# Local attention of a transformer step: strips of TensorE's array for the scores, one addition on GpSimd

## The reference, cut to what matters

```python
q = (x @ WQ_w + WQ_b).reshape(Bx, Lx, nh, d)
k = (x @ WK_w + WK_b).reshape(Bx, Lx, nh, d)
ak = (ax @ WK_w + WK_b).reshape(Bx, 1, nh, d)
av = (ax @ WV_w + WV_b).reshape(Bx, 1, nh, d)
pad_k = jnp.pad(k, ((0, 0), (1, 1), (0, 0), (0, 0)))
k_shift = jnp.stack([pad_k[:, t:Lx + t] for t in range(3)], axis=3)
K = jnp.concatenate([akb, k_shift], axis=3)
V = jnp.concatenate([avb, k_shift], axis=3)
scores = jnp.einsum('blhd,blhjd->blhj', q, K) / jnp.sqrt(jnp.float32(d))
alphas = jax.nn.softmax(scores, axis=-1)
att = jnp.einsum('blhj,blhjd->blhd', alphas, V).reshape(Bx, Lx, nh * d)
return att @ WO_w + WO_b
```

## Time and profile before

| | us |
|---|---|
| median of three runs | 1703.72 (1702.59 to 1705.21) |
| the profiled execution, its own time | 1703.39 |
| its span | 1701.6 |
| TensorE busy in the span | 1564.6 (92%) |
| VectorE busy | 827.5 (49%) |
| ScalarE busy | 662.9 (39%) |
| GpSimd busy | 94.7 (6%) |

### The profile page before, as it was taken

The page is one execution under the profiler, slowest core; times in us unless marked ns, Lnnn a source line. Parts: engine busy times, 40 slices in busy tenths (PEclk is TensorE's granted clock), DMA queues, the critical chain, the costliest instruction groups (busy, mean ns, idle before and its releaser), DMA issues. The chain is left out here.

```text
span 1701.6 us, 32009 instructions
## 1 busy us (share of the span) xinstructions
PE 1564.6 (92%) x11861; PEld 1250.0 (73%) x11862; DVE 827.5 (49%) x2926; ACT 662.9 (39%) x2449; POOL 94.7 (6%) x135
## 2 busy tenths in 40 slices
PE   7999989879999899999999999879999999866995
PEld 5666555537777799999999999638888888753663
DVE  2777668755445334444444444473333333565223
ACT  3211112125555145555555455314344434523442
POOL 0000000000000000000000000010000000003662
PEclk9988889889999999999999999859999999967998
DMA  4000000000000300000000000010000000001113
GB/s 146 1 1 1 0 1 1 1 0 1 1 1 1 100 1 2 2 1 2 2 2 1 2 2 1 1 31 21 20 26 20 27 14 2 1 1 47 41 43 92
DMA packets 27731, 28.05 MB, mean 16 GB/s; under 512 B 2293, under 2 KB 22234, under 8 KB 27450
## 3 DMA queue, kind: packets, MB, share of 16 engines
q1 hardware_dynamic: 20970, 16.70, 3.4%
q0 software_dynamic: 2496, 5.12, 1.0%
q10 hardware_dynamic: 4112, 4.19, 0.8%
HBM read 21.35 MB, written 4.65 MB: 15 GB/s over the span
## 5 line engine op out<-in xcount | busy, mean ns | idle before, releaser
L1457 PE MATMUL spare<-identb 128*128 128x128 bf16 x3166 | 218.2, 219 | 0.0
L1457 PEld LDWEIGHTS spare<-identb 128*128 128x128 bf16 x3166 | 201.7, 103 | 4.3
L292 PE MATMUL sc<-headsel,prod 128*128 128x128 f32 x1024 | 164.6, 315 | 0.7 <-DVE prod L437 0.7
L292 PEld LDWEIGHTS sc<-headsel,prod 128*128 128x128 f32 x1024 | 142.6, 218 | 26.7 <-issue 24.3
L1055 DVE TENSOR_TENSOR_SCAN narg<-rz,pre_n 128x16 f32<-128x16 f32 x256 | 47.9, 187 | 219.9 <-PE pre_n L952 218.9
L990 ACT ACTIVATE ghid<-gh_ps,cols 128x128 f32<-128x128 f32 x512 | 144.3, 366 | 12.9 <-PE gh_ps L891 12.7
L891 PE MATMUL gh_ps<-hist,w 128*128 128x128 f32 x1024 | 137.5, 275 | 0.6 <-ACT ghid L990 0.6
L900 PE MATMUL gy_ps<-w2e,ghid 128*128 128x128 f32 x1024 | 136.8, 276 | 0.6
L900 PEld LDWEIGHTS gy_ps<-w2e,ghid 128*128 128x128 f32 x1024 | 124.4, 191 | 3.0 <-issue 3.0
L891 PEld LDWEIGHTS gh_ps<-hist,w 128*128 128x128 f32 x1024 | 126.0, 188 | 0.8 <-DVE hist L1063 0.8
L952 PE MATMUL pre_r<-hist,gru_w 128*128 128x128 f32 x512 | 118.1, 312 | 0.7 <-DVE hist L1063 0.5
(11 more groups left out here) (374 smaller groups left out, 2664.1 us busy)
## 6 DMA issues: line engine op xcount, KB each, us to landing
w<-in_L_ffn_W SPq DMA_DIRECT2D x1, 2048.0 KB, 9.6
raw<-in_L_ffn_wg SPq DMA_DIRECT2D x8, 256.0 KB, 2.9
raw<-in_L_ffn_wu SPq DMA_DIRECT2D x8, 256.0 KB, 2.8
raw<-in_L_ffn_wd SPq DMA_DIRECT2D x8, 256.0 KB, 2.7
wqkv<-in_L_attn_Wqkv SPq DMA_DIRECT2D x1, 1536.0 KB, 6.4
mrow<-mt SPq DMA_DIRECT2D x4, 256.0 KB, 2.4
y_top<-yrow SPq DMA_DIRECT2D x4, 256.0 KB, 5.4
y_next<-yrow ACTq DMA_DIRECT2D x4, 256.0 KB, 6.1
```

The source lines that it names most:

```text
L292: mm = nc.tensor.matmul(sc[:, :, :, :].rearrange("p i j h -> p (i j h)"), prod[u % 2][:, j, P * i:P * i + P], headsel[:, P - 2 * k:2 * P - ...
L1457: nc.tensor.matmul(spare[:, 0:P], n.identb[:, :], n.identb[:, :], start=True, stop=True)
```

## The change

The block is written anew. `x` is kept as `xB`, one batch after the other, so neighbours are adjacent columns. The work goes in 32 steps (`STEPS`): 4 groups of two batches (512 columns) by 8 chunks. Per step:

- One projection of queries and one of keys, 512 columns each.
- One VectorE product of 128x1536 elements, for three keys instead of four: the conditioning key is folded into the query weights once at the start (`cond_keys`, `gq`) and costs two multiplications of 256 columns a group (`cond_scores`).
- Three score multiplications (`scores`). Now `headsel`, 32 columns wide, is the loaded operand and the product the moving one with 512 columns. Each writes its own strip of 32 partitions of one PSUM tile, `sc`, and so uses its own 32 columns of the array. All 8 chunks add to the same tile.
- The softmax comes once a group, for all 16 heads: ScalarE copies the scores to SBUF, TensorE turns them (`turn_scores`), VectorE works on 64 to 256 elements a partition, TensorE turns the parts back (`turn_probs`).
- Three spreads of 512 columns with 96, 96 and 48 rows, three VectorE terms (`weighted`), 10 steps behind the scores (`LAG`), so the loop has 43 rounds: 10 without spreads, 22 with everything (the last two of them without projections) and 11 with spreads and output alone.
- GpSimd adds two of the terms (`pair_terms`). The third goes to TensorE by itself: `project_out` makes two multiplications of 512 columns a step, with the same weights. The conditioning value's term is folded into the output weights (`av_wo`), two multiplications of 256 columns a group.

In the linear attention only the source of the residual `x` changes. The core of the diff:

```diff
+                    nc.scalar.activation(n.xB[:, 512 * g:512 * g + 512], turn[g % 2][:, :, :].rearrange("p i t -> p (i t)"),
...
-    HALF = TOK // 2
-    HB = HALF // P
-    SH = B
-    KW = HALF + 2 * SH
-    UNITS = 2 * NC
-    J = 4
+    J = 3
+    GB = 2
+    W = GB * T
+    NG = B // GB
+    STEPS = NG * NC
+    LAG = NC + 2
+    NK = LAG + 2
+    R = 32
+    HR = HEADS
...
+        headsel = sb("headsel", [P, 2 * R])
+        pick = sb("pick", [2 * 3 * HR, J, NC, 2, HD], BF16)
...
+        pj = [ps(f"pj{i}", [P, W]) for i in range(2)]
+        bc = [ps(f"bc{i}", [P, W]) for i in range(2)]
+        sc = ps("sc", [P, W])
+        y_ps = ps("y_ps", [P, W])
+        tok = ps("tok", [P, W])
+        tr = ps("tr", [2 * 3 * HR, 2, W], BF16)
...
+                def pair_terms(u):
+                    if not 0 <= u < STEPS:
+                        return
+                    pool.wait_ge(term_done, J * u + 2)
+                    if u >= 2:
+                        pool.wait_ge(y_part, u - 1)
+                    nc.gpsimd.tensor_tensor(pair[u % 2][:, :], term[u % 2][:, 0, :], term[u % 2][:, 1, :],
+                                            ALU.add).then_inc(pair_done, 1)
+
+                for u in range(STEPS):
+                    pair_terms(u)
...
+                def project(s, i):
+                    if s >= STEPS:
+                        return
+                    g, c = divmod(s, NC)
+                    k = 2 * s + i
+                    if k >= 2:
+                        pe.wait_ge(proj_kept, k - 1)
+                    w = (wq, wk)[i]
+                    nc.tensor.matmul(pj[k % 2][:, :], w[:, P * c:P * c + P], n.xB[:, W * g:W * g + W],
+                                     start=True, stop=True).then_inc(proj_done, 1)
...
+                def scores(s, j):
+                    if s >= STEPS:
+                        return
+                    g, c = divmod(s, NC)
+                    if j == 0 and c == 0 and g >= 1:
+                        pe.wait_ge(sc_kept, GB * g)
+                    if j == 0:
+                        pe.wait_ge(prod_v, s + 1)
+                    at = R * (j + 1)
+                    mm = nc.tensor.matmul(sc[at:at + R, :], headsel[:, R - 2 * c:2 * R - 2 * c], prod[s % 2][:, j, :],
+                                          start=(c == 0), stop=(c == NC - 1))
+                    if j == J - 1:
+                        mm.then_inc(score_done, 1)
...
+                def turn_scores(g):
+                    pe.wait_ge(sc_kept, GB * (g + 1))
+                    if g == 0:
+                        pe.wait_ge(gcol_kept, 1)
+                    else:
+                        pe.wait_ge(p0_kept, g)
+                    for i in range(4):
+                        mm = nc.tensor.transpose(tok[:, P * i:P * i + P], sc_sb[:, P * i:P * i + P], n.ident[:, :])
+                    mm.then_inc(sc_turned, 1)
...
+                def turn_probs(g):
+                    pe.wait_ge(parts_done, g + 1)
+                    if g >= 1:
+                        pe.wait_ge(turned_kept, g)
+                    for i in range(4):
+                        nc.tensor.transpose(tr[:, 0, P * i:P * i + P],
+                                            parts[:, J * i:J * i + 2, :, :].rearrange("p j k r -> p (j k r)"), n.identb[:, :])
+                        nc.tensor.transpose(tr[0:3 * HR, 1, P * i:P * i + P],
+                                            parts[:, J * i + 2, :, :].rearrange("p k r -> p (k r)"), n.identb[:, :])
+                    for i in range(4):
+                        mm = nc.tensor.transpose(tok[0:HEADS, P * i:P * i + P], prob0[:, i, :], n.ident[:, :])
+                    mm.then_inc(turned, 1)
...
+                def spread_probs(u, j):
+                    if not 0 <= u < STEPS:
+                        return
+                    g, c = divmod(u, NC)
+                    k = J * u + j
+                    if j == 0 and c == 0:
+                        pe.wait_ge(turned_kept, g + 1)
+                    if k == 0:
+                        pe.wait_ge(const_a, 10)
+                        pe.wait_ge(av_kept, 2)
+                    if k >= 2:
+                        pe.wait_ge(term_done, k - 1)
+                    k0 = 2 * 3 * HR if j < 2 else 3 * HR
+                    nc.tensor.matmul(bc[k % 2][:, :], pick[0:k0, j, c, :, :].rearrange("r h d -> r (h d)"),
+                                     probT[0:k0, j // 2, :], start=True, stop=True).then_inc(spread, 1)
+
+                def project_out(u):
+                    if not 0 <= u < STEPS:
+                        return
+                    g, c = divmod(u, NC)
+                    if c == 0:
+                        if g >= 1:
+                            pe.wait_ge(y_kept, g)
+                        else:
+                            pe.wait_ge(wav_kept, 1)
+                        pe.wait_ge(p0_kept, g + 1)
+                        for i in range(GB):
+                            nc.tensor.matmul(y_ps[:, T * i:T * i + T], av_wo[:, GB * g + i, :], p0T[:, T * i:T * i + T],
+                                             start=(i == 0), stop=False)
+                    pe.wait_ge(term_done, J * (u + 1))
+                    nc.tensor.matmul(y_ps[:, :], wo[:, c, :], term[u % 2][:, J - 1, :], start=False, stop=False)
+                    pe.wait_ge(pair_done, u + 1)
+                    nc.tensor.matmul(y_ps[:, :], wo[:, c, :], pair[u % 2][:, :], start=False,
+                                     stop=(c == NC - 1)).then_inc(y_part, 1)
...
+                for s in range(STEPS + LAG + 1):
+                    u = s - LAG
+                    project(s + 2, 0)
+                    spread_probs(u, 0)
+                    project(s + 2, 1)
+                    spread_probs(u, 1)
+                    project_out(u - 1)
+                    spread_probs(u, 2)
...
+                    if s % NC == 0 and 1 <= s // NC <= NG:
+                        turn_scores(s // NC - 1)
+                    scores(s, 0)
+                    scores(s, 1)
+                    scores(s, 2)
+                    if s % NC == NC - 1 and s < STEPS:
+                        cond_scores(s // NC)
+                    if s % NC == 1 and 1 <= s // NC <= NG:
+                        turn_probs(s // NC - 1)
...
+                def product(s):
+                    if s >= STEPS:
+                        return
+                    dve.wait_ge(proj_kept, 2 * (s + 1))
+                    if s >= 2:
+                        dve.wait_ge(score_done, s - 1)
+                    one = kb[:, s % NK, :, 0:T]
+                    three = bass.AP(one.tensor, one.offset, [one.ap[0], (1, J), *one.ap[1:]])
+                    q = qb[s % 3][:, :].rearrange("p (b t) -> p b t", b=GB).unsqueeze(1).broadcast_to([P, J, GB, T])
+                    nc.vector.tensor_tensor(prod[s % 2][:, :, :].rearrange("p j (b t) -> p j b t", b=GB), q, three,
                                             ALU.mult).then_inc(prod_v, 1)
...
+                def weighted(u, j):
+                    if not 0 <= u < STEPS:
+                        return
+                    k = J * u + j
+                    dve.wait_ge(spread, k + 1)
+                    if u >= 2 and j == 0:
+                        dve.wait_ge(y_part, u - 1)
+                        dve.wait_ge(pair_done, u - 1)
+                    nc.vector.tensor_tensor(term[u % 2][:, j, :].rearrange("p (b t) -> p b t", b=GB),
+                                            bc[k % 2][:, :].rearrange("p (b t) -> p b t", b=GB),
+                                            kb[:, u % NK, :, j:j + T], ALU.mult).then_inc(term_done, 1)
...
+                    if split:
+                        soft_sum(g)
+                    weighted(u, 0)
+                    if split:
+                        soft_reciprocal(g)
+                    weighted(u, 1)
+                    if split:
+                        soft_scale(g)
+                    product(s + 1)
+                    if split:
+                        part_high(g)
...
+                    if g is not None and at == 0:
+                        soft_max(g)
+                    weighted(u, 2)
+                    if split:
+                        part_rest(g)
+                        part_middle(g)
+                    if g is not None and at == 0:
+                        soft_shift(g)
+                    if split:
+                        part_last(g)
+                        part_low(g)
...
-                    nc.vector.scalar_tensor_tensor(x, out_ps[:, :], n.cols[:, bout:bout + 1], x,
+                    nc.vector.scalar_tensor_tensor(x, out_ps[:, :], n.cols[:, bout:bout + 1], n.xB[:, T * b:T * b + T],
```

More of the change, by code:

```diff
@@ new lines, in local_attention @@
+        rest1, rest2 = sb("rest1", [P, 4 * J, HR]), sb("rest2", [P, 4 * J, HR])
+        parts = sb("parts", [P, 4 * J, 3, HR], BF16)
+        probT = sb("probT", [2 * 3 * HR, 2, W], BF16)
+        p0T = sb("p0T", [HEADS, W])
```

(52 more changed lines are left out.)

438 lines of the change are left out of this document (198 added, 240 removed).

## The result

The changed kernel takes 1583.92 us (median of 4 runs, 1581.95 to 1589.98), against 1703.15 us before in the same comparison: ratio 0.9313, 95% interval 0.9275 to 0.9351. The profiled execution took 1589.98 us with a span of 1588.2, so 113.4 us less span than before. It was the slowest of the four, which lie 8 us apart, and its granted clock was 0.949 against 0.953 to 0.955 in the others.

A forecast was written before the change was run, and what follows sets the result against it. TensorE was taken to bound the block; its priced stretches summed to 272.5 us behind 13.4, so `yB` at 285.9 instead of 370.9, and 1703.4 - 85.0 gave 1618 us, range 1585 to 1655.

The forecast's parts named there:

- a full round: TensorE's round with projections, outputs, spreads, changes of division and scores: 3.44 + 0.69 + 0.40 + 1.72 = 6.25 us.
- conditioning scores, a group: TensorE, once per group: 4 passes of 256 columns and a change, 1.1 us.
- the price of the three score multiplications: TensorE, each step: second pass of a strip waits for its first, beside the next strip's first; 1.72 us.
- rival B: All three score strips run together, 0.86 us a step: kernel 1594 us, about 1600 with the skill's factor; chance 0.16.
- The middle: Scores at 1.72 us, between bounds 0.86 and 2.58, from pass order; own range 1606 to 1631 us, chance 0.42.
- signs named: `yB` at 275 to 300 us, projections every 6.2, six passes 1.7, additions 1.29, one wait near 2 each eighth round.
- Rival A: Score strips don't overlap on TensorE, 2.58 us a step: kernel 1643 us; chance 0.28.
- Rival C: Strips and changes of division keep TensorE's clock low: 1770 us with two thirds at half clock, 1848 at most; chance 0.04.
- Rival D: VectorE or the chain through it sets full rounds at 7.5 to 8.5 us: kernel 1644 to 1664; chance 0.10.
- Softmax waits: TensorE waits 1.8 us for VectorE's parts in rounds s = 9, 17, 25: parts at about 8.0, TensorE at 6.25.
- GpSimd's addition: One f32 addition a round, 1.29 us, slack 4.9, no matmul waiting; contention with the product, 4 us, only in the range.
- The changes of division: TensorE, each full round, into the 48-row spread, on to strips and back: bounds 0 and 0.9, taken as 0.40 us.

The follow-up runs named there:

- experiment 1: Changed kernel with the score multiplications, conditioning scores included, made at full 128-column width without strips: 1626.69 us, ratio 0.958 to the kernel before.
- experiment 5: Changed kernel with 13 instead of 12 key buffers (`NK`), the addition still on GpSimd: 1584.24 us, ratio 0.9309 to the kernel before.
- experiment 7: Changed kernel with `LAG` 11 instead of 10, `turn_probs` and ScalarE's copies one round later: 1571.32 us, ratio 0.9261 to the kernel before.
- experiment 3: Changed kernel with the addition of two terms moved from GpSimd to VectorE, behind the second term: 1592.65 us, ratio 0.9377 to the kernel before.
- experiment 6: Changed kernel with GpSimd's addition made twice, one behind the other, before telling TensorE: 1588.16 us, ratio 0.9329 to the kernel before.

## Why the prediction was wrong in size and right in kind

| step | forecast | measured |
|---|---|---|
| start of the loop | 27.3 | 28.24 |
| a round without spreads | 3.74 | 2.90 |
| round 10 starts | 78.3 | 72.30 |
| a full round | 6.25 | 5.38 |
| the scores in it, with the change back | 1.72 and a part of 0.40 | 0.99 |
| a round without projections | 4.53 | 3.56 |
| softmax wait in groups 0 to 2 | 1.8 | 2.48, 3.15, 3.15 |
| turning the parts | 2.0 | 2.3 |
| conditioning scores, a group | 1.1 | 0.01 to 0.02 |
| round 32 starts | 236.9 | 209.45 |
| from there to `yB` complete | 49.0 | 47.8 |

**The step that failed is the price of the three score multiplications**, "4 slots of 0.43 = 1.72". It was to say that the second pass of a strip waits for its first and holds the others up. It doesn't hold them up: first passes go together, then second passes, as the starts at 60.22 and 60.67 show. At the price of rival B, 0.86, the sum is 32 x 0.86 = 27.5 us shorter, which is all but 1 us of the 28.6. That the rest is so small is luck, since larger errors cancel in it. The sum was too long by 4.4 for the conditioning scores, which run beside the others in the fourth strip and cost almost nothing; by 1.8 for output multiplications in round 10, which has none; and by 1.2 in the tail. It was too short by 0.9 at the start, 3.4 in the softmax waits, 1.2 for the wait for the key copy, 0.9 in turning the parts and 3.4 for the half clock from 40 to 48 us, which no row had announced. The clock from 60 to 200 us took 8.4 us of work where 7.5 were forecast. Some 4 us more that the sum had too much, in smaller items, were not taken apart. The bounds of the scores were 0.86 and 2.58, and both can now be seen: 0.99 with the change in the result, 2.68 in experiment 1. The middle was an argument about order with no row behind it, and it was given the most weight; the measured end lay in a rival at 0.16.

Of the signs named, `yB` between 275 and 300 us, rounds of 6.2, six passes in 1.7 and additions of 1.29 failed, the first three on rival B's side; the one wait in eight rounds came. Full rounds stayed far under 7.2 us, and the clock away from the softmax waits at 1.00, but for the stretch from 40 to 48 us and the round at 77 us (11.32, experiment 5).

**Rival A** (no overlap) is experiment 1: 1626.69, where 1643 was named. Its round is 6.97 for 6.25 + 0.86 = 7.11, which is 4.5 us of the 16 between; the rest, waits and clock above all, was not taken apart. **Rival C** (low clock) is wrong for strips and their changes: in the stretch from 60 to 200 us the granted clock was 0.94, and 1.00 once the softmax wait was gone (experiment 7), with all changes of division in place. What took the clock down at 40 us stays open. **Rival D** (VectorE's chain) is wrong for the change as made, since its full rounds hold no wait, but for one key copy. But a chain of this kind was one step away: experiment 3 set it off by 0.69 us of VectorE work, through the key ring, which the prediction did not look at.

**Softmax waits** were forecast at the right place and too small, 2.48 to 3.15 for 1.8. In the middle groups part of it is that TensorE is there 0.8 us sooner, as B said, and the rest that the parts come about 8.55 us after the round's start for 8.0. The first group, s = 9, was priced wrongly on both sides: with a lag of 10 it has no terms and no spreads, so TensorE is there after 3.0 us and not 6.25, and the parts after 5.4 and not 8.0. VectorE's small operations, priced from a row of 64 adjacent elements, are longer: the sum of four takes 0.58 for 0.43, the reciprocal 0.55 for 0.30:

```profile
65.04 0.58 DVE L602 TENSOR_REDUCE s_sum<-s_exp 128x64 f32<-128x256 f32 x1 [0.48 <-ACT s_exp L495]
65.66 0.55 DVE L607 RECIPROCAL s_rec<-s_sum 128x64 f32<-128x64 f32 x1
```

and in the two middle groups GpSimd holds the product to 2.83.

**GpSimd's addition** was expected at 1.29 with no one waiting. No one waits in a full round, which experiment 6 shows by doubling it; its own time is 2.72. The rule cited beside the sum (the Trainium skill, GPSIMD Engine Reference, Key points) holds here: the product with two inputs in SBUF contends, the term with one in PSUM keeps its 0.68 to 0.69. The worst worked out for it, product and addition one after the other, is what happens. For it 4 us were kept in the range; the product was held up by 1.08 us in two softmax rounds and the cast by 0.95 in the last, 3.1 together, and what of that reaches the time was not measured by itself.

**The changes of division** (0.43 for 0.40), projections, spreads, outputs and the tail came out as worked out from starts in the trace of before.

## What to carry over

Where a cost has two bounds and no row between, give the mechanism at each bound its own weight and don't let an argument for a middle take over; a figure measured for a near case, here the 2.38x that the Trainium skill (TensorE: Matmul & The Clock Gate, Part 3) reports, deserved more than a rival's chance. Narrow matmuls paid here only where those of different strips stood next to each other in the program: three together 0.99 us, one alone 0.98. When the engine that bounds a kernel gets faster, look at what its producers can deliver next, here the softmax's parts (one more round of lag brought another 13 us), and at the depth of every ring whose reader and writer are in one round.

## What the runs showed of the hardware

- Three f32 multiplications of 512 columns in three column strips take 0.99 us where three of full size take 2.68, and two of 256 columns in the fourth strip go with them (start at 60.23, the round 0.02 longer). Each of the two passes overlaps across strips (starts at 60.22 and 60.67). With full-size multiplications between them each takes 0.97 to 0.98 alone.
- A spread of 96 rows takes 0.22 us, as one of full size was priced; one of 48 rows takes 0.31 and adds 0.10 ahead of it. Going to strips and back adds about 0.1 on each side.
- VectorE's product, with two inputs in SBUF, and its cast of 192 elements from f32 to bf16, with a single input, take turns with GpSimd's addition, and the later one is late: the addition takes 2.72 for 1.29, the product 2.83 for 1.75, the cast 1.20 for 0.25. VectorE's terms, with one input in PSUM, are not touched (0.63 to 0.69 throughout).
- In this block, idle stretches of TensorE of 2.5 to 4 us were each followed by the 1.2 GHz level; without them the clock stood at 1.00 for 140 us (experiment 7), with waits of 1.19 and 1.34 in it. It also fell at 40 us, without idle time in the 16 us before, and in the trace of experiment 7 did not.
